# Moving six operands of VectorE into PSUM, a ring of two for Q, and another mix of counts and weights on GpSimd's queue

## What is computed

```
h = relu(layernorm(x))
# layer 0, the one that the change is about
messages = concat(h[src], edge_rep[dst]) @ W1             # z, one row per edge
messages = relu(batch_norm over all edges (messages))
edge_new = segment_sum(messages, dst)                     # per destination
aggregate = segment_sum(edge_new[dst], src)               # = counts matrix @ edge_new
out0 = bn_relu(bn_relu((h + aggregate) @ W2a) @ W2b)
# layer 1: three rounds of  out += relu((0.1 * A_norm @ out + 0.9 * x0) @ conv_w[l])
# layer 2: attention over four heads of one edge per node; layer 3: gated sum over the edges
```

## Time and profile before

| | us |
|---|---|
| three runs: median (lowest to highest) | 3859.84 (3853.86 to 3864.0) |
| profiled execution: time / its span | 3863.74 / 3862.0 |
| DVE busy, share of the span | 2253.0, 58% |
| POOL busy, share of the span | 1959.2, 51% |
| PE busy, share of the span | 2421.3, 63% |

### The profile page before, as it was taken

How to read it: one execution, slowest core, us unless ns; L and a number is a source line. 1 busy time by engine, 2 the same in 40 slices (tenths; PEclk the granted TensorE clock), 3 DMA queues, 4 the chain that set the end, 5 groups by cost and what they waited for, 6 DMA issues and landing times. The chain is left out here.

```text
span 3862.0 us, 38365 instructions
## 1 busy us (share of the span) xinstructions
PE 2421.3 (63%) x11894; PEld 1975.4 (51%) x11894; DVE 2253.0 (58%) x4205; ACT 1351.2 (35%) x2765; POOL 1959.2 (51%) x1293
## 2 busy tenths in 40 slices
PE   5787444444444357730079973004999999982999
PEld 4422244444444345530069742004898889872688
DVE  6899577777777788840044432002555564545788
ACT  4488344444443200000033340002344434433576
POOL 0258888888888877777776677672000000015000
PEclk9888655555555578875589976557999999975999
DMA  9992355555555756631167411114555546513255
GB/s 352 353 293 25 50 163 169 164 164 169 165 168 166 160 164 186 188 74 0 0 175 179 89 1 0 0 0 114 171 170 149 172 132 183 171 29 74 72 173 177
DMA packets 339434, 521.99 MB, mean 135 GB/s; under 512 B 144970, under 2 KB 226691, under 8 KB 332195
## 3 DMA queue, kind: packets, MB, share of 16 engines
q1 hardware_dynamic: 197144, 446.27, 35.7%
q0 software_dynamic: 135920, 61.61, 13.8%
q10 hardware_dynamic: 6170, 11.66, 1.0%
HBM read 370.82 MB, written 148.58 MB: 134 GB/s over the span
## 5 line engine op out<-in xcount | busy, mean ns | idle before, releaser
L1051 PE MATMUL ps<-rows_r,lhs_r 128*128 128x448 f32 x3500 | 901.7, 372 | 594.5 <-DVE ring_r L495 300.1
L1051 PEld LDWEIGHTS ps<-rows_r,lhs_r 128*128 128x128 f32 x3500 | 666.2, 190 | 668.9 <-issue 583.9
L666 POOL DMA_INDIRECT counts<-wts x391 | 738.6, 1889 | 371.0 <-issue 205.2
L675 POOL DMA_INDIRECT weights<-wts x391 | 651.2, 1666 | 239.8 <-issue 237.1
L495 DVE SCALAR_TENSOR_TENSOR ring_r<-ring,dinv,rows_r 128x896 fp32r<-128x896 f32 (+1 forms) x300 | 303.6, 1033 | 613.5 <-ACT rows_r L483 613.5
L683 POOL DMA_INDIRECT reg<-tab_p,w x440 | 500.3, 1137 | 136.7 <-issue 132.7
L1051 PE MATMUL ps<-ring_r,lhs_r 128*128 128x448 f32 x1750 | 527.8, 371 | 0.0
L483 ACT ACTIVATE rows_r<-ring,dinv 128x896 fp32r<-128x896 f32 (+1 forms) x300 | 284.8, 951 | 687.8 <-PE ps L1051 353.4
L729 POOL DMA_INDIRECT el<-tab_l,base_i x25 | 24.0, 958 | 819.5 <-DMA tab_l<-reg 812.2
L493 DVE TENSOR_TENSOR ring_r<-ring,rows_r 128x896 fp32r<-128x896 f32 x200 | 191.9, 972 | 354.6 <-ACT rows_r L481 354.3
L1051 PEld LDWEIGHTS ps<-ring_r,lhs_r 128*128 128x128 f32 x1750 | 333.8, 191 | 31.1
(11 more groups left out here) (247 smaller groups left out, 3835.3 us busy)
## 6 DMA issues: line engine op xcount, KB each, us to landing
ring<-weights SPq DMA_DIRECT2D x225, 448.0 KB, 3.3
ring<-counts SPq DMA_DIRECT2D x150, 448.0 KB, 3.3
zbuf<-reg SPq DMA_DIRECT2D x220, 256.0 KB, 2.9
reg<-zbuf SPq DMA_DIRECT2D x55, 1024.0 KB, 4.7
counts<-ring SPq DMA_DIRECT2D x25, 1568.0 KB, 15.8
weights<-ring SPq DMA_DIRECT2D x25, 1568.0 KB, 17.8
ring<-cells SPq DMA_DIRECT2D x38, 448.0 KB, 4.0
ring<-weights SPq DMA_DIRECT2D x75, 224.0 KB, 3.2
```

Source lines behind the costliest of these rows:

```text
L666: pool.indirect_dma_start(counts, bass.IndirectOffsetOnAxis(ap=ix_c[:, k:k + 1], axis=0), vals_c[:, k:k + 1], None, compute_op=ALU.add).th ...
L675: pool.indirect_dma_start(weights, bass.IndirectOffsetOnAxis(ap=ix_w[:, k:k + 1], axis=0), vals_w[:, k:k + 1], None, compute_op=ALU.add).t ...
L1051: m = pe.matmul(bank[:, 0:BLK], lhs[part], rows[:, c:c + BLK], start=first, stop=last)
```

## The change

Four things move on the chip, and one number changes in a queue.

- The eight PSUM banks become one tensor, `banks`. The mask of `equal_cells`, the row of the maximum (`nb_ps`) and the column numbers (`cols_ps`) are read from PSUM instead of SBUF, after one copy each; `zacc` lies in PSUM, is read and written there, and is copied to SBUF (`zsum`) once at the end.
- To make room, the Q ring shrinks from four banks to two: `add_q(q)` now waits for `add_z(q-2)` instead of `add_z(q-4)`.
- `group_totals` has one bank instead of two: it waits for `group_cells` of the group before instead of the one before that.
- `W_MID` goes from 2 to 5.

```diff
-W_FROM, W_PER, W_MID = 42, 4, 2
+W_FROM, W_PER, W_MID = 42, 4, 5
...
-        zacc = view(F0 + 24 * H, 4 * H)
+        zsum = view(F0 + 24 * H, 4 * H)
...
-        mask = view(F0 + 44 * H, NG * P)
-        at = F0 + 44 * H + NG * P
+        at = F0 + 44 * H
...
-        ps = [ctx.enter_context(nc.psum_tensor(f"ps{k}", [P, 512], F32)) for k in range(8)]
-        deg_bank, tot_bank, stat_bank, sort_bank = ps[0], (ps[1], ps[2]), ps[3], (ps[4], ps[5])
+        banks = ctx.enter_context(nc.psum_tensor("banks", [P, 8 * 512], F32))
+        ps = [banks[:, k * 512:(k + 1) * 512] for k in range(8)]
+        deg_bank, tot_bank, stat_bank, sort_bank = ps[0], ps[1], ps[4], (ps[4], ps[5])
+        mask, cols_ps = banks[:, 2 * 512:2 * 512 + NG * P], banks[:, 2 * 512 + NG * P:4 * 512]
+        nb_ps, zacc = ps[2][:, 0:H], banks[:, 6 * 512:8 * 512]
...
             def group_totals(g):
-                wait(pe, cells_ready, g - 1)
+                wait(pe, cells_ready, g)
...
-                        m = pe.matmul(tot_bank[g % 2][:, 4 * y:4 * y + 4], s[:, o:o + P], cw4[:, g * NG + xk, :],
+                        m = pe.matmul(tot_bank[:, 4 * y:4 * y + 4], s[:, o:o + P], cw4[:, g * NG + xk, :],
...
             def add_q(q):
-                if q >= 4:
-                    pe.wait_ge(z_ready, q - 3)
+                if q >= 2:
+                    pe.wait_ge(z_ready, q - 1)
...
-                        m = pe.matmul(ps[4 + q % 4][:, k % 2 * H:(k % 2 + 1) * H], oT[q // 4 % 2][:, k % 8 * P:(k % 8 + 1) * P],
+                        m = pe.matmul(ps[4 + q % 2][:, k % 2 * H:(k % 2 + 1) * H], oT[q // 4 % 2][:, k % 8 * P:(k % 8 + 1) * P],
...
-            pe.wait_ge(z_acc, KQ)
+            pe.wait_ge(z_acc, KQ + 1)
...
+            do(v.tensor_copy(cols_ps, cols[:, :]))
             do(v.memset(mask[:, 0:(NG - 1) * P], 1.0))
...
             sum_z(KQ - 1)
+            v.wait_ge(z_acc, KQ)
+            v.tensor_copy(zsum, zacc).then_inc(z_acc, 1)
...
+            do(v.tensor_copy(nb_ps, nb_row[:, :]))
...
             def destinations(i):
-                v.tensor_tensor(hot_d[i % 2], cols[:, :].unsqueeze(1).to_broadcast([P, 8, P]), bcast(s_low[:, 8 * i:8 * i + 8], P),
+                v.tensor_tensor(hot_d[i % 2], cols_ps.unsqueeze(1).to_broadcast([P, 8, P]), bcast(s_low[:, 8 * i:8 * i + 8], P),
...
             def messages(i):
-                v.tensor_tensor(zin[i % 3], zin[i % 3], nb_row[:, :].unsqueeze(1).to_broadcast([P, 8, H]),
+                v.tensor_tensor(zin[i % 3], zin[i % 3], nb_ps.unsqueeze(1).to_broadcast([P, 8, H]),
```

More of the change, by code:

```diff
@@ L1158, in _ @@
                     o = (2 * part + k) * H
-                    m = pe.matmul(stat_bank[:, part * H:(part + 1) * H], ones[:, :], zacc[:, o:o + H], start=(k == 0), stop=(k == 1))
+                    m = pe.matmul(stat_bank[:, part * H:(part + 1) * H], ones[:, :], zsum[:, o:o + H], start=(k == 0), stop=(k == 1))
             m.then_inc(stat_done, 1)
@@ L1162, in _ @@
             for j in range(JH):
[L1163 removed]
+                m = pe.transpose(ps[5][:, j * P:(j + 1) * P], absg[:, j * P:(j + 1) * P], ident[:, :])
             m.then_inc(a_cols, 1)
@@ L1399, in one_hots @@
                 wait(v, lanes_ready, 8 * (i - 1))
-                v.tensor_tensor(unit_hot[i % 2][:, :].rearrange("p (k e) -> p k e", k=8), cols[:, :].unsqueeze(1).to_broadcast([P, 8, P]),
+                v.tensor_tensor(unit_hot[i % 2][:, :].rearrange("p (k e) -> p k e", k=8), cols_ps.unsqueeze(1).to_broadcast([P, 8, P]),
                                 bcast(lane[:, 8 * i:8 * i + 8], P), ALU.is_equal).then_inc(unit_ready, 1)
@@ L1414, in degree_rows @@
                 cs, h = slice(8 * i, 8 * i + 8), hw[i % 2]
-                do(v.tensor_tensor(h[:, :, NT:2 * NT], cols[:, 0:NT].unsqueeze(1).to_broadcast([P, 8, NT]), bcast(t_hi[:, cs], NT),
+                do(v.tensor_tensor(h[:, :, NT:2 * NT], cols_ps[:, 0:NT].unsqueeze(1).to_broadcast([P, 8, NT]), bcast(t_hi[:, cs], NT),
                                    ALU.is_equal))
@@ L1482, in add_z @@
                 k = 2 * q % 8
-                v.tensor_tensor(zz[q % 4][:, 0:2 * H], ps[4 + q % 4][:, :],
+                v.tensor_tensor(zz[q % 4][:, 0:2 * H], ps[4 + q % 2],
                                 gp[:, k:k + 2, :].rearrange("p a c -> p (a c)"), ALU.add).then_inc(z_ready, 1)
```

6 lines of the change are left out of this document (3 added, 3 removed).

## The result

The changed kernel takes 3750.12 us (median of 4 runs, 3742.93 to 3759.34), the kernel before 3856.85 (4 runs, 3840.65 to 3864.0): a ratio of 0.973, interval 0.9691 to 0.977. The profiled execution has a span of 3752.5 us. Between the medians lie 106.7 us, where 128 were forecast (3859.84 to 3732). Forecast were 3732, with 3692 to 3790 as range and 3705 to 3760 as the likeliest case's own.

A forecast was written before the change was run, and what follows sets the result against it. GpSimd's queue, held by DVE instructions with two large SBUF sources, was taken as the bound. Sort -11, gather passes -38 and message passes -84 made -133 us from 3863.74, adjusted to the median and rounded to 3732; range 3692 to 3790.

The forecast's parts named there:

- any DVE stream this long holds the queue: Rival: a PSUM source doesn't free GpSimd's queue, nothing is gained, bank and ring costs remain; 3897 us, chance 0.04.
- The sort: Stretch before the gathers: 18 us of queue excess, 7 left for small instructions; -11 us.
- The message passes: Stretch behind the gather passes: only the queue counts, so its whole excess goes and landing waits stay; -84 us.
- W_MID: Weights ahead of the last count: counts end 164 us later, covered by PE's 300 us idle; no time change.
- The gather passes: Gather stretch: shorter passes -71, totals bank +32, ring +5, end -4; -38 us in all.
- The single bank of totals: Long gather passes: PE waits for group_cells of the group before, 0.85 us in each of 38; +32 us.
- The ring of two: End of short gather passes: loads wait for the third pair's add_z, mostly covered by ACT; 15 x 0.3, +5 us.
- PSUM as destination: sum_z in the gather passes: writing PSUM costs nothing; upper bound 0.15 us each, 33 us over 55 passes.
- the loop takes the gather stretch: Rival: PSUM destination costs 33 us, the ring 15 not 5, so gather passes give +5; 3771 us, chance 0.22.
- The queue's wins whole: Rival: gather passes keep the queue's full gain, PE's wait being hidden and passes falling to floors; 3695 us, chance 0.10.
- counts as the bound: Rival: later counts delay dense(0) and its successors until dense(1) waits for PE; 3762 us, chance 0.04.
- compares not reached: Rival: equal_cells' pointer scalars in SBUF still hold the port, so sort and some gather excess stay; 3750 us, chance 0.03.

The follow-up runs named there:

- e1: Kernel before with one edit: the message passes' maximum reads its row from PSUM, after one added copy; 3828.84 us, ratio 0.9858.
- e7: Changed kernel with the sums of z back in SBUF and a ring of four for Q; 3799.4 us, ratio 0.9791.
- c1: Changed kernel run again, unedited, as a control in a later group; 3797.31 us, ratio 0.977 to the kernel before.
- c3: Changed kernel run again, unedited, in the last group; 3830.64 us, ratio 0.9863 to the kernel before.
- c2: Kernel before run again, unedited, for a second trace in the last group; one execution, 3889.22 us.
- e2: Changed kernel with W_MID back from 5 to 2; 3842.7 us, ratio 0.988 to the kernel before.
- e4: Changed kernel with a ring of four for Q again, mask and column numbers back in SBUF; 3860.31 us, ratio 0.9924.
- e6: Changed kernel with group_cells of a long pass moved to the start of the next pass on DVE; 3781.73 us, ratio 0.9743.
- e5: Changed kernel with a long pass's group_totals moved behind the second add_q of the next pass; 3792.71 us, ratio 0.9766.
- e8: Changed kernel with C_PER of 0, so no counts between the gathers, all behind them; one execution, 4018.17 us.
- e9: Changed kernel with a long pass's group_totals moved behind the fourth add_q of the next pass; 3807.45 us, ratio 0.9804.

## Why the prediction was right, and where it was not

**The bound** was named rightly. What follows the last weight starts when GpSimd's queue has ended, and DVE's maximum with two SBUF sources held the queue: with one source in PSUM the count beside it takes 1.55 us, and e1 shows it by that operand alone. The rival that any DVE stream this long holds the queue (3897 us) is refuted by the same row, and so is the Trainium skill's inference (page "SBUF — State Buffer", section "Who interferes with whom") for operands that all lie in SBUF: e7's gathers with `sum_z` in SBUF take 1114 ns, c1's 969 and c3's 965.

**The sort**: -11 forecast, -12.4 measured, -11.2 in c3. The counts went from 1864 to 1560 ns; the weights did not come down, 1797 ns for 1723. Over 1546 ns that leaves 45 x 0.014 + 27 x 0.251 = 7.4 us, which is the 7 that were left for the small instructions.

**The message passes**: -84 forecast. The stretch from last gather to last weight gives -72.4. The queue in that stretch, before and after (length, busy us and count, PE's granted clock, DMA engines' busy share, GB/s):

```profile
1347.13:2639.23 1292.10, 949.01 (x544) 0.73 0.39 80
```

```profile
1319.07:2538.81 1219.74, 861.56 (x543) 0.74 0.42 85
```

Its busy time fell by 87.4 us, so the excess was sized well; each DMA came down to 1546 ns beside the message passes. Its idle time rose from 343.1 to 358.2, by 15.1 us, and that is the mis-sized step: "the waits for landings come from the transfers beside them and stay". Beside the message passes idle time grew from 70.1 us before 103 DMAs to 101.8 before 136, 0.68 to 0.75 us each. This growth doesn't repeat: from c2 to c3 the busy time fell by 81.0 us, the idle time rose by 3.6, and a DMA beside the message passes has 0.69 us of it in both. So the step held in the second pair of traces, and why it didn't in the first is not shown.

**W_MID**: nothing forecast, and nothing found. 131.90 us of cover left, where 130 was written; e2 shows the 163 us on the counts and 1.0 us on the weights. The last count came at 2004 where 1970 was written: the 22 us that the gather passes, and the 12 that the message passes, gave less than forecast.

**The gather passes**: -38 forecast, -15.7 from first to last gather, and this is the miss. By its steps:
- The loop was seen as the limit, rightly: the queue now waits 109.7 us for buffers. Of the 16 long passes after short ones most run at the loop's pace; five (1, 11, 18, 38 and 52) still wait for gathers, and only pass 52 by much, 22.53 us.
- The single bank of totals was put at 0.85 us in each long pass. Long passes after long ones went from 17.64 to 18.42: 0.78. The rows are as written, the last one of `group_cells` on DVE, and 0.05 us behind its end the totals on PE, then `add_q` with the 2.18 us that nothing hides, as in the earlier trace rows:

```profile
869.91 0.16 DVE L1444 TENSOR_TENSOR wts<-fin,consts 128x7 int32<-128x7 f32 x1
```

```profile
870.12 0.91 PE L1097 MATMUL banks<-cw,same 128*128 128x4 bf16 x28 [8.25 <-DVE wts L1444]
873.21 0.58 PE L1138 MATMUL banks<-lhs_r,oT 128*128 x1 [2.18 <-issue]
```

- The ring of two was put at 0.3 us in 15 passes, "mostly covered by ACT", **and this step failed**. The floor of a long pass after a short one was set at 16.5 us because its second `add_z` came 1.73 us behind the first. With two pairs PE isn't ahead there: its `add_q` for that pass starts late, ACT's work with it, and the second `add_z` comes 2.83 us behind, as in every other pass. PE, and DVE's first two `add_z` of pass 25:

```profile
854.82 0.57 PE L1138 MATMUL banks<-lhs_r,oT 128*128 x1 [2.66 <-issue]
```

```profile
856.24 0.69 DVE L1487 TENSOR_TENSOR reg<-banks,reg 128x512 f32<-128x512 f32 x1
...
859.07 0.68 DVE L1487 TENSOR_TENSOR reg<-banks,reg 128x512 f32<-128x512 f32 x1
```

  So the floor is 17.65 and not 16.5 us, and the pass takes 18.42 with the totals, where 17.65 was forecast. By these rows the ring's price is 1.1 us in 15 passes and 0.25 in the 15 short ones, 20 us for 5. The delays are shown: with four pairs the second `add_z` comes after 1.73 us in e7 and 2.08 in e4, and short passes take 9.53 in both. That the long passes end 1.1 us later for it is argued from the first trace alone. In e4 and e7 the long passes after short ones took 23.3 and 20.2 us, lengthened by the wait that no view names.

For the first pair of traces the miss is then counted out. Between the first `add_z` of pass 0 and that of pass 54 lie 868.1 us instead of 880.9 (-13), where -34 was forecast (-71 + 32 + 5). The long passes after long ones gave +16.7 (forecast 22 x 0.85 = 18.7), the short ones +0.5, and the 15 after short ones -29 instead of -52. These 23 us are 15 x 0.77 = 12 for the floor, 7 for the passes that still wait for gathers, and 4 because these passes took 20.8 us in the trace before and not the 21.1 that the prediction's subtraction left. The last gather comes 5.0 us ahead of that `add_z` and not 2.2, so -3 for the -4.

**PSUM as destination**: taken as nothing, with 0.15 us as upper bound on each `sum_z`. Measured 1231 ns for 1221, 0.01 us:

```profile
L1497 DVE TENSOR_TENSOR banks<-banks,reg 128x1024 f32<-128x1024 f32 x219 | 269.6, 1231 | 47.9 <-ACT reg L843 47.9
```

The Trainium skill's extra for a PSUM source (page "VectorE: DVE Perf Modes", section "The TRN2 errata") doesn't show: the maximum went from 2.29 to 2.28 us with its second source there.

**The sum**: the three stages of the forecast give -12.4 - 15.7 - 72.4, some -100 for -133, and the stage behind the last weight, for which nothing was forecast, gave -9.1 between the two traces, of which c2 and c3 repeat 2.7. So about 30 us of 133 were not there; by the medians 21 are missing (106.7 for 128). A small slip of arithmetic stands in the sum as well: 3731 - 3.9 is 3727, not 3728.

**What was luck.** The mechanism was right, but that the time fell into the range is owed in part to when it was measured. In the other groups the change was worth 85.4 and 53.4 us, with 3797.31 and 3830.64 us, both above 3790; the kernel before was slower there too, by some 26 us. Off the kernel before's 3859.84, 53.4 us less would be 3806. The prediction has no term for what makes the difference, long passes after short ones of 18.42, 20.86 and 22.94 us.

**The rivals**: of "the loop takes the gather stretch" a part came true, by the rows of the ring and not by the PSUM destination, and the time stayed inside the likeliest case's range. The queue's wins whole, counts as the bound and compares not reached are out by the rows above (for the compares: the counts of the gather passes take 1627 ns for 1962).

## What to carry to other kernels

When a queue is held up by another engine's operands, sum the excess over its quiet duration, but grant a stretch only what the loop beside it leaves: here 72 of 84 us came where only the queue counted, and 16 of some 117 where a loop of three engines ran at nearly the same pace. Pay for the PSUM that such a move takes with the order of instructions, and price a shorter ring at the pass where the engines' lead used to be made good, not inside a steady pass: moving `group_cells` alone (e6) gave 15.6 us back between the medians, at the edge of what four runs can tell. And take a second trace at another time before building on a gain: three traces of one kernel had the same passes at 18.42, 20.86 and 22.94 us, and the gain of the whole change was 106.7, 85.4 and 53.4 us.

## What the runs showed of the hardware

**A wait that no view names.** In c1 and c3, and strongest in e5, e8 and e9, ACT and DVE go on waiting for PE when PE's rows of that work are over: up to 2.6 us in c1, 7 in e9. "remote" or "issue" stands as releaser. In c1 all 15 long passes after short ones (pass 1 left out) have their next `add_z` start 0.69 to 1.12 us behind the end of the queue's last row; in the first trace of the same kernel it starts at will while the queue is in the middle of its burst. The last row of the burst in c1's pass 28, and the `add_z` behind it:

```profile
944.92 1.61 POOL L669 DMA_INDIRECT counts<-wts  x1 [0.30 <-issue]
```

```profile
947.37 0.69 DVE L1487 TENSOR_TENSOR reg<-banks,reg 128x512 f32<-128x512 f32 x1 [3.57 <-PE banks L1138]
```

e8 shows that it needs no counts in the burst, and that it may come inside a pass; in c3 it is the fourth `add_z`, at 9.04 us of the pass instead of 6.40. In e8 it ends when the transfers of gathers and of z have nearly run out. That gathered rows land late is excluded for these waits: by the DMA packets the last one of the gathers ended 7.5 us before the `add_z` that waits in e8, and 2.9 before the one in c3 (medians of 15). That PE itself is held by the transfers, and its rows are written too early, would fit; so would a signal that comes late. Neither was shown. The kernel before has a small form of it in c2, 1.1 us in ten of its 22 long passes after long ones. Why its long passes after short ones are spared (4.63 to 4.79 us behind the compares in all 15) is open as well. The queue is busy for 0.81 of the time in those passes of c2, for 0.69 in c3's and 0.39 in e8's, so a busy queue is not what makes the wait long. The gather passes of c3 are 38 us longer than c2's, and 36.5 of these us lie in the 15 long passes after short ones.

**A PSUM operand frees the queue at almost no cost on DVE.** Beside the same 128x2048 maximum of 2.28 us a DMA of the queue takes 3.45 us with both sources in SBUF (a weight) and 1.55 with one in PSUM (a count); by `sum_z` alone gathers go from 1114 ns (e7) to 969 (c1), and DVE pays 10 ns for the PSUM destination.
